# AdaLN, Mamba scan and mixture of experts on one core: the next batch's statistics and its normalization move into the stretch behind scan 2, with scan 3 behind the router's logits

## The chip, the cores and the metric

The kernel runs on one NeuronCore of a Trainium2 chip. The metric is the device time of one execution in microseconds; the kernel is run several times and the median is compared.

Its engines are named as the profile names them: PE (TensorE, matrix products and transposes; PEld are its weight loads), DVE (VectorE), ACT (ScalarE), POOL (GpSimd) and SP (SyncE, which here only issues DMAs). Each engine works through its own queue in order; semaphores tie the queues together.

## The reference

Eight batches of x, 512 rows by 128 columns, all in float32. Each goes through

```python
h = layernorm(x) * (1 + ca) + sa
x = x + ga * mamba(h)
h = layernorm(x) * (1 + cb) + sb
x = x + gb * moe(h)
```

where sa to gb come from a small conditioning product. The Mamba part is

```python
xz = h @ in_proj.T; x, z = split(xz)
u = silu(causal_conv(x) + conv_b)              # 256 channels
dt, Bm, Cm = split(u @ x_proj.T)               # 8 + 16 + 16 columns
delta = softplus(dt @ dt_w.T + dt_b)
s = s * exp(delta * A) + (delta * u) * Bm      # 16 states per channel, over 512 steps
y = sum_n(s * Cm) + u * D
out = (y * silu(z)) @ out_proj.T
```

The expert part has a shared expert and 8 routed ones, of which the two with the highest router probability count, weighted by it:

```python
probs = softmax(flat @ router_w + router_b)
weights = probs where among the top 2, else 0   # a tie goes to the lower index
out = shared(flat) + sum_e weights[e] * expert_e(flat)   # each: gelu(x @ w1 + b1) @ w2 + b2
```

## The kernel before

**Pipeline.** `pipeline` (L293) calls each engine's `slots(b, a, n, m)` for stretches i = 0 to 7. In stretch i the engines scan batch b = i, finish batch a = i − 1 (gate, output projection, experts), prepare batch n = i + 1 (convolution, dt, softplus), and normalize the x of batch m = i + 2. So a and m are both there in stretches 1 to 5; stretch 0 has no a, stretches 6 and 7 have no m. A prologue comes before, a `tail` for the last batch behind.

**Units.** The scan of a batch is 16 units u of 128 partitions by 1024 elements (two states of one half of the channels). For each, VectorE makes the input (`scan_input`, L1197: B row times delta·u, into PSUM), then runs the scan (`scan`, L1206). GpSimd multiplies by C (`readout`, L433), TensorE adds the result to y by transposes (`y_add`, L516). ScalarE makes the decay factors (`decays`, L885, two instructions per unit). Scan u waits for decay u, for its input, and for `y_add` of unit u − 4, whose state buffer it takes (`STATE_RING` 4). `AHEAD` says how many units' decays are made in the stretch before.

**VectorE's queue.** The order is written by hand in `slots` (L1318). Between the units stand the jobs of the other batches:
- `gate_y(a)`, L1216;
- `residual(a)` (L1222: adds attention's rows in PSUM to x, then the statistics of the second normalization);
- `x1hat(a)` (L1238: normalizes; waits for `rstd2_done`);
- `split_h2(a)`, L1310, and `logits(a)` (L1249, three small instructions; waits for the router's product);
- `top2(a)`, L1264, which makes the weights;
- `stats(m)` (L1144; waits for the load of x, `x_in`) and `xhat(m)` (L1155; waits for `rstd_done`);
- `make_delta(n)` (L1163, softplus' sums) behind scan 7, `delta_x(n)` behind scan 12.

**GpSimd's queue.** `slots` (L437) has the last readout of a, then readouts 0 to 14 of b. A readout that is `paced` also waits until the input of the unit after next scan, u + 1, is made. `make_rstd` (two tiny instructions, L420 and L423: add epsilon, power −0.5; called the root below) stands behind readout 2 for a and behind readout 5 for m.

**TensorE's queue** (L700). After the output projection: dt_proj 0, `att_transpose(a)` (L600), dt_proj 1, `y_add` 0 and 1, `keep_busy` (transposes of the identity with no use for the result, L611), `x1_transpose(a)` (L616), `y_add` 2, `keep_busy`, `router(a)` (L624), 18 `up` projections (L645 to L647; the first waits for the split), `y_add` 3, and then `down` products and mixes with the further `y_add`s.

**ScalarE's queue** (L1017). softplus' steps, `softplus_exp`, decays, `h2_rows(a)` (L992, L995: the transposed x1 scaled, read by the split and the router), decays, `router_e`, 18 gelus, `softplus_log`, then mixes and decays in turn.

**SP's queue** (L354). `load_x(m)` (L347) stands behind the store of n's B and C rows to DRAM (L361) and the wait for its landing; these stand behind the end of the preceding stretch. At the end of stretch 1 that is the one-time store of the gate row, and a wait for it:

```python
if b and b.i == 1:
    sp.wait_ge(gate_steps, 4)
    sp.dma_start(gate_dram, gateT[:, 1, B - 1:B]).then_inc(gate_stored, 16)
    sp.wait_ge(gate_stored, 16)
```

**Top 2.** Five instructions of 128 by 256 elements: other = mine, other > mine, the former times a mask of lower indices (`before`), the sum of both, and its reduction to a rank.

## Time and profile before

| what | us |
|---|---|
| median of 3 runs | 687.32 |
| lowest and highest | 684.01, 691.07 |
| the profiled execution | 684.8 |
| its span | 683.1 |
| VectorE busy in it | 598.3 |
| TensorE busy | 593.3 |
| ScalarE busy | 489.7 |
| GpSimd busy | 320.2 |

The profile covers one execution. The span runs from the first to the last recorded instruction; the profiled execution's own time is 1.7 us longer. Times of rows count from the span's start.

### The profile page before, as it was taken

What the parts mean: (1) busy time and instruction counts of PE and PEld (TensorE: products, weight loads), DVE (VectorE), ACT (ScalarE), POOL (GpSimd) and SP (SyncE); (2) the same over time, 40 slices, a digit from 0 to 9 for tenths busy, and PEclk for the clock granted to TensorE, in tenths of its full rate; (3) what the DMA queues carried; (4) which work ended last, traced back from release to release, by engine and by line L of the source; (5) the groups of instructions that cost most, each with busy time, mean ns of one, the idle gap of its engine ahead of it and who ended that gap; (6) DMA issues with size and microseconds to landing.
All of it is one profiled execution on the core that took longest, in us unless ns stands there. A gap on an engine that the chain in (4) does not pass through costs nothing.

```text
span 683.1 us, 9767 instructions
## 1 busy us (share of the span) xinstructions
PE 593.3 (87%) x3646; PEld 466.5 (68%) x3646; DVE 598.3 (88%) x713; ACT 489.7 (72%) x861; POOL 320.2 (47%) x171
## 2 busy tenths in 40 slices
PE   5684478899989998999989998999979947998897
PEld 4243345689657965788567966787668936798686
DVE  5399999999999999999999999999998999798416
ACT  3689535999589976989589957998598925962460
POOL 1036556446654556446653656446543664464000
PEclk9787589999999999999999999999999968999999
DMA  7423333314432235133531343223522442220000
GB/s 221 161 92 140 123 139 142 125 70 169 163 128 82 108 128 184 62 124 124 173 124 63 124 160 138 83 103 124 179 103 70 176 156 83 103 78 16 1 1 16
DMA packets 26705, 77.87 MB, mean 114 GB/s; under 512 B 3025, under 2 KB 17570, under 8 KB 18466
## 3 DMA queue, kind: packets, MB, share of 16 engines
q1 hardware_dynamic: 26178, 76.82, 31.1%
q8 instruction: 29, 0.48, 0.3%
q10 hardware_dynamic: 480, 0.43, 0.2%
q14 instruction: 18, 0.15, 0.1%
HBM read 74.61 MB, written 2.62 MB: 113 GB/s over the span
## 4 chain that ended last, share of the span: by engine, by line
PE 53%; DVE 31%; issue 7%; ACT 5%; POOL 2%; DMA 1%; DVEq 0%; POOLq 0%; ACTq 0%
DVE state L1206 15%; PE psum L677 12%; PE psum L516 10%; DVE psum L1197 8%; PE psum L543 5%; PE psum L645 5%; PE psum L647 4%; PE psum L646 4%; PE psum L687 3%; POOL state L433 2%; PE psum L662 2%; PE psum L565 1%; ACT L866 1%; DVE out_sb L1244 1%; PE psum L799 1%
## 5 line engine op out<-in xcount | busy, mean ns | idle before, releaser
L433 POOL TENSOR_TENSOR state<-state,bc 128x1024 f32<-128x1024 f32 x127 | 300.1, 2363 | 291.8 <-DVE psum L1197 291.8
L1206 DVE TENSOR_TENSOR_SCAN state<-decay,psum 128x1024 f32<-128x1024 f32 x128 | 292.2, 2283 | 21.9 <-PE psum L516 9.5
L885 ACT ACTIVATE decay<-delta,a_neg 128x511 f32<-128x511 f32 x256 | 166.1, 729 | 10.4 <-DVE state L1206 10.3
L516 PE MATMUL psum<-ident,state 128*128 128x128 f32 x1024 | 139.0, 283 | 33.6 <-POOL state L433 33.4
L1197 DVE TENSOR_TENSOR psum<-bc,du 128x1024 f32<-128x1024 f32 x128 | 157.6, 1231 | 4.8 <-DVE state L1206 0.5
L516 PEld LDWEIGHTS psum<-ident,state 128*128 128x128 f32 x1024 | 120.3, 146 | 56.0 <-POOL state L433 44.9
L677 PE MATMUL psum<-down_w,h 128*128 128x128 f32 x896 | 109.9, 276 | 0.0
L677 PEld LDWEIGHTS psum<-down_w,h 128*128 128x128 f32 x896 | 104.4, 192 | 5.3 <-issue 5.3
L1014 ACT ACTIVATE h<-psum,vec 128x512 f32<-128x512 f32 x144 | 97.0, 688 | 2.1 <-PE psum L647 0.6
L980 ACT ACTIVATE gT_mix<-psum,w 128x128 f32<-128x128 f32 x224 | 64.8, 388 | 20.0 <-PE psum L687 14.4
L645 PE MATMUL psum<-h_hi,up_hi 128*128 128x512 f32 x144 | 59.2, 411 | 10.7 <-DVE h_lo L1310 6.7
L543 PE MATMUL psum<-h_sb,conv_in_wT 128*128 128x512 f32 x128 | 59.9, 614 | 8.8 <-ACT h_sb L895 8.8
L647 PE MATMUL psum<-h_hi,up_lo 128*128 128x512 f32 x144 | 57.7, 401 | 0.0
L646 PE MATMUL psum<-h_lo,up_hi 128*128 128x512 f32 x144 | 57.6, 400 | 0.0
L543 PEld LDWEIGHTS psum<-h_sb,conv_in_wT 128*128 128x128 f32 x128 | 24.3, 199 | 34.6 <-issue 25.4
L645 PEld LDWEIGHTS psum<-h_hi,up_hi 128*128 128x128 f32 x144 | 27.5, 191 | 20.5 <-DVE h_lo L1310 7.3
L687 PE MATMUL psum<-ident,gT_mix 128*128 128x128 f32 x224 | 33.9, 274 | 0.0
L647 PEld LDWEIGHTS psum<-h_hi,up_lo 128*128 128x128 f32 x144 | 27.4, 190 | 6.7
L646 PEld LDWEIGHTS psum<-h_lo,up_hi 128*128 128x128 f32 x144 | 27.6, 191 | 6.0
L687 PEld LDWEIGHTS psum<-ident,gT_mix 128*128 128x128 f32 x224 | 26.0, 141 | 1.5 <-ACT gT_mix L980 1.5
L611 PE MATMUL psum<-ident 128*128 128x128 f32 x210 | 26.2, 273 | 0.0
L906 ACT ACTIVATE du<-psum,vec 128x512 f32<-128x512 f32 x16 | 10.8, 687 | 21.2 <-PE psum L543 18.7
(151 smaller groups left out, 638.3 us busy)
## 6 DMA issues: line engine op xcount, KB each, us to landing
bc<-bc_rows SPq DMA_DIRECT2D x64, 1024.0 KB, 4.7
x_sb<-_attn_hidden_states_dram SPq DMA_DIRECT2D x9, 256.0 KB, 2.8
x<-_attn_hidden_states_dram SPq DMA_DIRECT2D x7, 256.0 KB, 3.0
out_dram<-out_sb SPq DMA_DIRECT2D x7, 256.0 KB, 2.4
h<-in_L_ffn_rw_dram SPq DMA_DIRECT2D x1, 1024.0 KB
bc_rows<-rows SPq DMA_DIRECT2D x8, 64.0 KB, 4.8
h<-in_L_wmod_dram ACTq DMA_DIRECT2D x1, 384.0 KB
h<-in_L_attn_in_proj_w_dram SPq DMA_DIRECT2D x1, 256.0 KB, 4.7
```

Source lines behind the costliest of these rows:

```text
L433: pool.tensor_tensor(state[:, u % STATE_RING, :, :], state[:, u % STATE_RING, :, :], bc[:, pair % BC_RING, 1, first:first + NU, :], ALU.mu ...
L516: last = nc.tensor.matmul(Y[q][:, t * P:(t + 1) * P], state[:, u % STATE_RING, s, t * P:(t + 1) * P], ident[:, :], start=False, stop=(u in ...
L543: last = nc.tensor.matmul(A[q], conv_in_wT[:, q, k, :], h_sb[:, k:k + L], start=(k == 0), stop=(k == KC - 1))
L645: nc.tensor.matmul(bank, high, h2_hi[:, :], start=True, stop=False)
L646: nc.tensor.matmul(bank, high, h2_lo[:, :], start=False, stop=False)
L647: nc.tensor.matmul(bank, low, h2_hi[:, :], start=False, stop=True).then_inc(up_done, 1)
L677: last = nc.tensor.matmul(A[j % 2][:, e * DM:(e + 1) * DM], h1[:, (group * EG + e) * HQ + q, ts], down_w[:, group * EG + e, q, :], start=( ...
L687: last = nc.tensor.matmul(OUTP[:, t * P:(t + 1) * P], mix[:, j % 2, e, :], ident[:, :], start=False, stop=(j == DOWNS - 1 and e == EG - 1) ...
L885: last = nc.scalar.activation(decay[:, r, s, 1:L], delta[:, b.p, q, 1:L], ACT.Exp, scale=a_neg[:, q, k:k + 1])
L1014: nc.scalar.activation(h1[:, m, :], UP_RING[m % 3], ACT.Gelu, bias=vec[:, bias:bias + 1]).then_inc(gelu_done, 1)
L1197: nc.vector.tensor_tensor(IN, bc[:, pair % BC_RING, 0, first:first + NU, :], du[:, b.p, q:q + 1, :].broadcast_to([P, NU, L]), ALU.mult).th ...
L1206: nc.vector.tensor_tensor_scan(state[:, u % STATE_RING, :, :].rearrange("p n t -> p (n t)"), decay[:, u % DECAY_RING, :, :].rearrange("p n ...
```

## The change

On VectorE, where both a and m are there, `stats(m)` moves from ahead of scan 6 to behind `residual(a)`, and `xhat(m)` from behind scan 6 to behind input 3. `x1hat(a)` stands ahead of input 3, and split and logits ahead of scan 3. Without m the order of a's jobs changes alike; without a nothing does. The two statistics get buffers of their own (`bn_in`).

On GpSimd readout 2 isn't paced where there is an a, and the root for m follows the one for a. On TensorE `att_transpose` comes ahead of dt_proj 0, `y_add` 2 ahead of `x1_transpose`, and `keep_busy` has other counts. On ScalarE seven units' decays are made ahead, and one fewer pair before the gelus. `top2` has three large instructions, not five: mine is scaled by 1 − 2^-24 where the other's index is lower, and one comparison counts both kinds.

```diff
-AHEAD = 6
+AHEAD = 7
...
         bn = sb("bn", [P, NT, 6])
+        bn_in = sb("bn_in", [P, NT, 6])
...
                     if b:
-                        readout(b, u)
+                        readout(b, u, paced=not (a and u == 2))
                     if a and u == 2:
                         make_rstd(1, stats2_done, rstd2_eps, rstd2_done, a)
-                    if m and u == 5:
+                    if m and u == (2 if a else 5):
                         make_rstd(0, stats_done, rstd_eps, rstd_done, m)
...
+                if a:
+                    att_transpose(a)
                 if n:
                     dt_proj(n, 0)
-                if a:
-                    att_transpose(a)
-                if n:
                     dt_proj(n, 1)
...
-                if a:
-                    keep_busy(a, n, 14)
+                    y_add(b, 2)
+                if a:
+                    keep_busy(a, n, 8)
                     x1_transpose(a)
-                if b:
-                    y_add(b, 2)
-                if a:
-                    keep_busy(a, n, 5 if b else 12)
+                    keep_busy(a, n, 10)
                     router(a)
...
                 if b:
                     decays(b, AHEAD)
+                if a:
+                    h2_rows(a)
+                if b:
                     decays(b, AHEAD + 1)
-                if a:
-                    h2_rows(a)
-                if b:
-                    decays(b, AHEAD + 2)
-                    decays(b, AHEAD + 3)
...
-                    if b and j < DOWNS - 2:
-                        decays(b, AHEAD + 4 + j)
+                    if b:
+                        decays(b, AHEAD + 2 + j)
...
-                nc.vector.tensor_tensor(gt_eq[:, 1, :, :, :], other, mine, ALU.is_equal
-                                        ).then_inc(prob_step, 1)
-                nc.vector.tensor_tensor(gt_eq[:, 0, :, :, :], other, mine, ALU.is_gt
-                                        ).then_inc(prob_step, 1)
+                nc.vector.tensor_tensor(
+                    gt_eq[:, 1, :, :, :], pr[:, :, :].unsqueeze(3).broadcast_to([P, NT, E, E]),
+                    tie_scale[:, :, :].unsqueeze(1).broadcast_to([P, NT, E, E]),
+                    ALU.mult).then_inc(prob_step, 1)
+                dve.wait_ge(prob_step, k + 4)
+                nc.vector.tensor_tensor(
+                    gt_eq[:, 0, :, :, :], pr[:, :, :].unsqueeze(2).broadcast_to([P, NT, E, E]),
+                    gt_eq[:, 1, :, :, :], ALU.is_gt).then_inc(prob_step, 1)
                 dve.wait_ge(prob_step, k + 5)
-                nc.vector.tensor_tensor(
-                    gt_eq[:, 1, :, :, :], gt_eq[:, 1, :, :, :],
-                    before[:, :, :].unsqueeze(1).broadcast_to([P, NT, E, E]),
-                    ALU.mult).then_inc(prob_step, 1)
-                dve.wait_ge(prob_step, k + 6)
-                nc.vector.tensor_tensor(gt_eq[:, 0, :, :, :], gt_eq[:, 0, :, :, :],
-                                        gt_eq[:, 1, :, :, :], ALU.add).then_inc(prob_step, 1)
...
                     scan_input(b, 2)
                     scan(b, 2)
+                if a:
+                    residual(a)
+                if a and m:
+                    stats(m)
+                if a:
+                    x1hat(a)
                 if b:
                     scan_input(b, 3)
-                if a:
-                    residual(a)
+                if a and m:
+                    xhat(m)
+                if a:
+                    split_h2(a)
+                    logits(a)
                 if b:
                     scan(b, 3)
-                if a:
-                    x1hat(a)
-                if b:
                     scan_input(b, 4)
                     scan(b, 4)
-                if a:
-                    split_h2(a)
-                    logits(a)
-                if b:
                     scan_input(b, 5)
                     scan(b, 5)
                 if a:
                     top2(a)
                 if b:
                     scan_input(b, 6)
-                if m:
+                if m and not a:
                     stats(m)
                 if b:
                     scan(b, 6)
-                if m:
+                if m and not a:
                     xhat(m)
```

## Rows read from the trace of the kernel before

**Rows 1.** The page: busy us of each engine (share); the scans (busy, mean ns | idle before).

```profile
PE 593.3 (87%) x3646; PEld 466.5 (68%) x3646; DVE 598.3 (88%) x713; ACT 489.7 (72%) x861; POOL 320.2 (47%) x171
...
L1206 DVE TENSOR_TENSOR_SCAN state<-decay,psum 128x1024 f32<-128x1024 f32 x128 | 292.2, 2283 | 21.9 <-PE psum L516 9.5
```

**Rows 2.** Timeline of VectorE in stretch 4: start, duration, line, operation.

```profile
339.78 2.29 DVE L1206 TENSOR_TENSOR_SCAN state<-decay,psum 128x1024 f32<-128x1024 f32 x1
...
343.25 0.69 DVE L1226 TENSOR_TENSOR x<-psum,x 128x512 f32<-128x512 f32 x1
...
345.18 2.25 DVE L1206 TENSOR_TENSOR_SCAN state<-decay,psum 128x1024 f32<-128x1024 f32 x1
347.35 1.09 DVE L1244 TENSOR_SCALAR out_sb<-x,mean_var,rstd 128x128 f32<-128x128 f32 x4
...
351.92 0.67 DVE L1310 TENSOR_TENSOR h_lo<-h,h_hi 128x512 fp32r<-128x512 f32 x1
...
353.05 1.23 DVE L1197 TENSOR_TENSOR psum<-bc,du 128x1024 f32<-128x1024 f32 x1
...
356.61 0.16 DVE L1268 TENSOR_REDUCE router_stats<-gT_mix 128x4 f32<-128x32 f32 x1
...
359.52 1.23 DVE L1197 TENSOR_TENSOR psum<-bc,du 128x1024 f32<-128x1024 f32 x1
360.65 0.86 DVE L1147 BATCH_NORM_STATS2 bn<-x_sb 128x6 f32<-128x128 f32 x4
...
361.85 2.26 DVE L1206 TENSOR_TENSOR_SCAN state<-decay,psum 128x1024 f32<-128x1024 f32 x1
364.51 1.12 DVE L1158 TENSOR_SCALAR x_sb<-x_sb,mean_var,rstd 128x128 f32<-128x128 f32 x4 [0.40 <-POOL rstd L423]
...
367.29 2.29 DVE L1206 TENSOR_TENSOR_SCAN state<-decay,psum 128x1024 f32<-128x1024 f32 x1 [0.52 <-PE psum L516]
...
375.29 2.29 DVE L1206 TENSOR_TENSOR_SCAN state<-decay,psum 128x1024 f32<-128x1024 f32 x1
...
378.98 2.29 DVE L1206 TENSOR_TENSOR_SCAN state<-decay,psum 128x1024 f32<-128x1024 f32 x1
```

**Rows 3.** Groups by line: one of top2's large instructions (count | busy, mean ns | idle before).

```profile
L1288 DVE TENSOR_TENSOR gT_mix<-gT_mix 128x256 f32<-128x256 f32 x8 | 3.4, 425 | 0.3
```

**Rows 4.** Timeline of GpSimd in stretch 4: readout 2 and the power of the root.

```profile
343.42 2.38 POOL L433 TENSOR_TENSOR state<-state,bc 128x1024 f32<-128x1024 f32 x1 [1.34 <-DVE psum L1197]
...
346.03 1.01 POOL L423 TENSOR_TENSOR rstd<-rstd,constants 128x4 f32<-128x4 f32 x1
```

**Rows 5.** Timeline of TensorE in stretch 4: attention's transpose and the router.

```profile
341.61 0.66 PE L600 MATMUL psum<-ident,h 128*128 128x128 f32 x4
...
350.69 1.06 PE L624 MATMUL psum<-router_sb,h 128*128 128x8 f32 x8
```

**Rows 6.** Timeline of SP's DMA issues; the page's row on x's loads (KB, us to landing).

```profile
183.78 0.43 SPq L385 DMA_DIRECT2D gate_row<-gateT  x1
193.36 0.32 SPq L387 DMA_DIRECT2D gate_row_sb<-gate_row  x1
...
198.81 0.38 SPq L347 DMA_DIRECT2D x_sb<-_attn_hidden_states_dram  x1
...
416.61 0.39 SPq L347 DMA_DIRECT2D x_sb<-_attn_hidden_states_dram  x1
...
x_sb<-_attn_hidden_states_dram SPq DMA_DIRECT2D x9, 256.0 KB, 2.8
```

**Rows 7.** Timeline of VectorE in stretch 2: scan 2.

```profile
189.56 2.29 DVE L1206 TENSOR_TENSOR_SCAN state<-decay,psum 128x1024 f32<-128x1024 f32 x1
```

**Rows 8.** The page: the decays.

```profile
L885 ACT ACTIVATE decay<-delta,a_neg 128x511 f32<-128x511 f32 x256 | 166.1, 729 | 10.4 <-DVE state L1206 10.3
```

**Rows 9.** Two windows: length, busy of each engine, granted clock (PEclk), DMA share, GB/s.

```profile
546.00:552.00 6.00, 2.70 (x20) 2.14 (x20) 5.80 (x4) 4.33 (x7) 3.71 (x2) 1.00 0.08 33
552.00:560.00 8.00, 3.23 (x15) 2.69 (x14) 7.70 (x6) 0.00 (x0) 4.68 (x2) 0.55 0.58 194
```

## What the change should do to the time

> **What bounds the kernel now.** I first read the busy line of the page [rows 1]: VectorE (DVE) 598.3 us and TensorE (PE) 593.3 us of a span of 683.1 us. A share can't say which of the two holds the other, so I read VectorE's timeline of one period, the stretch in which batch 4 is scanned [rows 2]. Scan 2 ends there at 339.78 + 2.29 = 342.07 and scan 7 starts at 367.29, that is 25.22 us later. In between VectorE stands still only twice: 0.40 us ahead of the normalization of x (L1158), for GpSimd's root, and 0.52 us ahead of scan 7, for TensorE. The reader is to see that everything else on that engine touches: an instruction that waits for nothing starts some 0.08 us before the one ahead of it ends, a scan 1.36 us after the start of its own input (1.23 long). Five such pairs repeat at 3.69 us from scan to scan (375.29 to 378.98). For 16 units per batch that is 59 us of a period of 75.1 (from scan 2 of stretch 2, 189.56 [rows 7], to that of stretch 4, halved); the rest is side work on the same queue. So in the middle of the run VectorE is the bound, and a change is worth what it takes off VectorE's queue less what it makes that queue wait. The start and the end, where other engines set the pace, are untouched here.
>
> Eight stretches i = 0 to 7 scan one batch each. The change acts where a batch is finishing (a) beside one being scanned (b): i = 1 to 7. In i = 1 to 5 there is also a batch whose x is prepared (m); in 6 and 7 there is none. All times below count from the end of scan 2.
>
> **The change, part by part: a stretch with m.**
>
> *Residual.* attention's transpose (L600) ends at 341.61 + 0.66 = 342.27 behind half of dt_proj [rows 5]; put ahead of it, it ends about 0.2 earlier, at 0.0. The residual, formerly behind input 3, can start at 0.1. Its block lasts 345.18 − 343.25 = 1.93, so it ends at 2.04.
>
> *Next x's statistics.* They last 361.85 − 360.65 = 1.20 and reach 3.24.
>
> *The root.* GpSimd's readout 2 no longer waits for input 3 (it could not: input 3 now stands behind the root) and starts at 0.1. From a readout's start to the end of the root behind it is 346.03 + 1.01 − 343.42 = 3.62 [rows 4], so x1hat starts at 3.74. The statistics fill 1.2 of that wait and 0.5 remains: a wait that was not there.
>
> *Scan 3 behind split and logits.* Before, scan 4 and input 4 covered the way x1hat, transpose, h2, router, logits. The way takes from x1hat's start 347.35 to the router's end 350.69 + 1.06 = 351.75, i.e. 4.40, and 0.04 to wake VectorE [rows 2, 5]. What is left in front of logits is x1hat 1.00 (1.09 long, overlapped), input 3 1.13, xhat 1.03 (1.12) and the split 0.58 (0.67): 3.74. So split and logits wait 0.7 in all and logits start at 3.74 + 4.44 = 8.18. Split and logits together took 353.05 − 351.92 = 1.13, logits 0.55 of it, so scan 3 starts at 8.73. ScalarE has one pair of decays ahead of h2 rather than two, so h2 isn't held.
>
> *The rest.* Scans 4 and 5 at 12.42 and 16.11, top2 2.20 behind at 18.31. top2's block lasted 359.52 − 356.61 = 2.91. It loses one operation that overlapped its neighbour (0.42 − 0.08 = 0.34) and one that waited for its predecessor (0.425 + 0.04 = 0.46) [rows 3]: 0.80 less, so input 6 starts at 20.42, scan 6 at 21.79, scan 7 at 25.48. Scan 7 no longer waits for TensorE: the up projections start some 2.7 earlier, and so does the readout's sum behind them.
>
> Result: 25.48 against 25.22, **+0.26 per stretch**. The 0.80 of top2 and the 0.92 of two old waits are paid back by 1.2 of new ones, and by lost overlaps: three scans, not one, are followed directly by their next input, and one more scan stands directly behind its input. Bounds: −0.2 (both new waits 0.25 shorter), +0.5.
>
> *Decays.* AHEAD = 7 shifts one pair (2 × 0.729 = 1.5 at most, [rows 8]) from behind softplus to the end of the preceding stretch, and one more pair into the stretch of the mixes. There they are covered: ScalarE starts its gelus about 2 earlier. If that cover were gone, TensorE's chain to gate_y would be late by up to 1.5 per stretch. I take 0 and keep +0.5 per stretch for the range. keep_busy (14 + 5 becomes 8 + 10) lies in TensorE's idle time: 0.
>
> *Stretches 6 and 7.* Without m there is nothing to fill: x1hat still starts at 3.74, so scan 7 still at 25.48. Before, these two lacked 1.20 + 1.03 + 0.40 of work and wait, but stood for TensorE instead: of the 9.5 us for PE in seven waits [rows 1], five like the one shown leave 6.9 for these two, 3.4 each. So before they were at about 25.2 − 2.6 − 0.5 + 3.4 = 25.5. Change: 0, within ±1.5 for both.
>
> **Where the new order meets a transfer.** stats(m) used to run at 360.65, 18.6 us behind scan 2, and now at 2.04. It needs x, which SP loads only after it has stored and seen landed the B and C rows. I read SP's queue for each stretch [rows 6]. In stretch 2 (b.i = 1 came before) SP stood from 183.78 to 193.36 for the one-time store of the gate row, so x is issued at 198.81 and lands 2.8 later, at 201.6. Scan 2 ends there at 189.56 + 2.29 = 191.85 [rows 7]. x is there at 9.8, and VectorE wants it at 2.04. Queued behind it on VectorE are x1hat, input 3 and everything else. x1hat starts at 9.8 + 1.2 = 11.0 instead of 3.74: **+7.3**, once. The other four loads are issued earlier. The latest of them, at 416.61, lands at 419.4; scan 2 ends in that stretch one period (75.1) behind 342.07, so x is there at 2.3, 0.2 late, which the wait for the root covers.
>
> While VectorE stands, TensorE does too, for 7 us. In the trace TensorE was busy 2.70 of the 6 us up to 552, at a granted clock of 1.00 (2.4 GHz), and the mean over the next 8 us was 0.55, nearly all of it at the lower level, 1.2 GHz [rows 9]. A full stop of 7 us should do the same: then x1's transpose (0.66) and the router (1.06), both on the way to logits, take up to twice as long: up to 1.7, I take 1.2. The Trainium skill (TensorE: Matmul & The Clock Gate, § Part 1: The HAM clock gate) likewise says that an idle array falls back to 1.2 GHz; at a clock that stayed up, the sum would be 1.2 lower.
>
> **Sum.** 4 stretches × 0.26 = 1.0; stretch 2: 7.3 + 0.26 + 1.2 = 8.8; stretches 6 and 7: 0; start and end: 0 (in the end top2 is covered by TensorE's projections). **+9.8 us.** The profiled execution took 684.8 us, its span 683.1 with 1.7 around it; it becomes 694.6. That execution lies 2.5 below the median of the runs shown, 687.3, to which I add the same: **697.1 us**, 1.4% slower.
>
> **Rivals.**
>
> *GpSimd held by VectorE.* The root for x now runs beside x1hat and input 3. In the rows before, roots ran beside scans only ([rows 4] beside 345.18). If x1hat and input 3 hold GpSimd off, the power (1.01) starts at about 6.1, xhat at 7.15, split at 8.2, logits at 8.8, scan 3 at 9.35: +0.6 in five stretches, total +12.9: 700.2. For it: the code paces every readout to avoid input rows. Against it: operands of four elements. The Trainium skill (SBUF — State Buffer, § Who interferes with whom) says that a VectorE instruction with two SBUF inputs, or in a two-port mode, excludes a GpSimd instruction that reads SBUF. By that rule it comes out this way; no row here shows the overlap.
>
> *A shorter stop in stretch 2.* The gate row is 0.5 KB and landed 9.6 us after its issue [rows 6], once, in one execution. If in other executions it takes no longer than the x load, 2.8, x is there 6.8 earlier, at 3.0: the stop shrinks to 0.5 and the clock stays up. Total 5 × 0.26 + 0.5 = +1.8: 689.1. A landing of 6.5 gives +6.7, 694.0, the edge of what is within 1%. For it: the trace has this store once. Against it: nothing that runs ahead of it on SP is changed.
>
> *Gain.* If the way to logits were covered and x there in time in every stretch, the new waits of 0.5 + 0.7 go: 25.48 becomes 24.3, 0.9 below before: 5 × 0.9, and 0.8 of top2 in two more stretches: −6.1: 681.2, near the edge of faster by 1%. It decides on one row: x's load in stretch 2 must be there at 2.0, and 198.81 speaks plainly against it. Even without that stop, the root and router rows keep the balance at +1.
>
> *Late engines.* ScalarE's extra decays make TensorE's chain late by 0.5 in five stretches: +12.3: 699.6.
>
> **How the numbers follow.** Forecast (+8 to +11) 0.42; GpSimd held 0.20; late engines 0.08; shorter stop or none 0.18; gain 0.07; something else, split evenly, 0.05. About 1% is what a measurement of this kernel can tell from no change: 6.9 us, so the bounds are 680.4 and 694.2. Slower by over 1%: forecast, held and late, 0.70, of which the spread of runs takes a little and half of something else gives some back: 0.68. Faster: half of the gain case, and a part of something else: 0.05. Within 1%: the rest, 0.27. Range: the lower end holds the shorter stop with the spread of the runs shown (3.5), 690; the upper end the held case with it, 703.
>
> **What would show it.** In the profile after: the first instruction of x's statistics in stretch 2 waits some 7.5 us for the DMA of x; x1hat waits 0.5 for GpSimd and logits 0.5 for the router in stretches 1, 3, 4 and 5; no wait of scan 7 for TensorE; top2 2.1 long; the distance from scan 2's end to scan 7's start 25.5. If that wait in stretch 2 is missing, the forecast is wrong by its largest term. If the distance is 26 or more with xhat waiting for the root, the second case holds. If gate_y waits over 0.5 for TensorE, the decays were not hidden.

## The result, and the profile after

The changed kernel is slower: median 702.1 us (701.4 to 706.0, 4 runs) against 687.5 us (684.0 to 691.1) of the kernel before; ratio 1.0231, 95% interval 1.0187 to 1.0276, that is 15.9 us (12.9 to 19.0). I had forecast 9.8 us. The direction and its largest term were right; the size was too small by over a third.

The page of the changed kernel, busy us and scans, to be held against [rows 1]:

```profile
span 700.0 us, 9730 instructions
...
PE 602.8 (86%) x3639; PEld 474.9 (68%) x3639; DVE 595.5 (85%) x697; ACT 490.3 (70%) x861; POOL 320.1 (46%) x171
...
L1203 DVE TENSOR_TENSOR_SCAN state<-decay,psum 128x1024 f32<-128x1024 f32 x128 | 292.5, 2285 | 14.2 <-DVE psum L1194 0.5
```

VectorE has 2.8 us less to do, and the scans' idle time fell from 21.9 to 14.2 us: no scan 7 waits for TensorE now. Yet the span grew by 16.9 us. The groups of waits of VectorE say what it waits for instead (in total, times, longest; the large waits of start and end left out):

```profile
DVE bn_in L1144 <- DMA x_sb<-_attn_hidden_states_dram: 9.3, 2, 6.7
DVE h_lo L1301 <- ACT h_hi L994: 8.3, 7, 2.2
...
DVE gT_mix L1251 <- PE psum L626: 7.5, 8, 3.3
DVE out_sb L1241 <- POOL rstd L425: 5.9, 7, 1.6
```

In the kernel before, x's load held VectorE for 2.9 us in all, the router 3.3, the root ahead of x1hat 1.4, all in the start and the end, and h2 not at all. x's load (L1144), h2 (L1301), the router (L1251) and the root (L1241) are the four places at which the new order waits.

**Stretch 4** of the changed kernel, VectorE's timeline, answers [rows 2]. Scan 2 ends at 352.22 + 2.29 = 354.51.

```profile
352.22 2.29 DVE L1203 TENSOR_TENSOR_SCAN state<-decay,psum 128x1024 f32<-128x1024 f32 x1
354.61 0.69 DVE L1223 TENSOR_TENSOR x<-psum,x 128x512 f32<-128x512 f32 x1
...
358.22 1.12 DVE L1241 TENSOR_SCALAR out_sb<-x,mean_var,rstd 128x128 f32<-128x128 f32 x4 [0.42 <-POOL rstd L425]
359.25 1.23 DVE L1194 TENSOR_TENSOR psum<-bc,du 128x1024 f32<-128x1024 f32 x1
360.39 1.11 DVE L1155 TENSOR_SCALAR x_sb<-x_sb,mean_var,rstd 128x128 f32<-128x128 f32 x4
362.00 0.69 DVE L1301 TENSOR_TENSOR h_lo<-h,h_hi 128x512 fp32r<-128x512 f32 x1 [0.51 <-ACT h_hi L994]
363.12 0.19 DVE L1251 TENSOR_TENSOR gT_mix<-psum,router_bias 128x32 f32<-128x32 f32 x1 [0.43 <-PE psum L626]
...
363.67 2.29 DVE L1203 TENSOR_TENSOR_SCAN state<-decay,psum 128x1024 f32<-128x1024 f32 x1
...
380.48 2.29 DVE L1203 TENSOR_TENSOR_SCAN state<-decay,psum 128x1024 f32<-128x1024 f32 x1
```

x1hat starts 3.71 behind scan 2 (forecast 3.74), scan 7 starts at 380.48, 25.97 behind (forecast 25.48, before 25.22). The three waits are where the forecast put them: 0.42 for the root (forecast 0.5), and 0.51 + 0.43 = 0.94 ahead of split and logits together (forecast 0.7). logits start at 363.12 − 354.51 = 8.61, 0.43 later than forecast.

**Stretch 2**: SP's issues, to be held against [rows 6].

```profile
186.48 0.43 SPq L386 DMA_DIRECT2D gate_row<-gateT  x1
195.42 0.32 SPq L388 DMA_DIRECT2D gate_row_sb<-gate_row  x1
...
200.36 0.38 SPq L348 DMA_DIRECT2D x_sb<-_attn_hidden_states_dram  x1
```

VectorE's first instruction of x's statistics, in the timeline of the same stretch:

```profile
203.18 0.87 DVE L1144 BATCH_NORM_STATS2 bn_in<-x_sb 128x6 f32<-128x128 f32 x4 [6.68 <-DMA x_sb<-_attn_hidden_states_dram]
```

The chain of waits of that stretch (start, us, what), which goes back from the projections:

```profile
186.48 8.92 DMA gate_row<-gateT
...
195.78 4.56 DMA bc_rows<-rows
...
200.36 2.80 DMA x_sb<-_attn_hidden_states_dram
...
203.18 0.87 DVE bn_in L1144 x4
```

The three transfers follow each other with at most 0.4 between them, as the forecast had it. Scan 2 ended there at 194.38; scan 7 starts 33.29 behind it, 8.05 more than in the kernel before (25.24).

Stretch by stretch, the distance from scan 2's end to scan 7's start, from the two profiled executions (us):

| stretch | 1 | 2 | 3 | 4 | 5 | 6 | 7 |
|---|---|---|---|---|---|---|---|
| before | 25.24 | 25.24 | 25.23 | 25.22 | 25.23 | 25.42 | 26.70 |
| after | 28.13 | 33.29 | 27.64 | 25.97 | 25.98 | 25.98 | 26.47 |
| difference | 2.89 | 8.05 | 2.41 | 0.75 | 0.75 | 0.56 | −0.23 |

Together 15.2 of the span's 16.9 us. Stretches 1 and 3 stand out; the next view is theirs. Two pairs of windows of TensorE in the changed kernel, ahead of and around x1's transpose, stretch 3 and stretch 4 (length, busy of PE, PEld, DVE, ACT, POOL, granted clock, DMA share, GB/s):

```profile
272.00:279.00 7.00, 5.98 (x27) 3.12 (x25) 6.66 (x8) 4.40 (x8) 4.74 (x3) 1.00 0.31 110
279.00:283.00 4.00, 4.00 (x22) 3.90 (x22) 3.53 (x19) 3.97 (x7) 3.04 (x5) 0.59 0.00 0
```

```profile
349.00:356.00 7.00, 5.98 (x29) 3.36 (x27) 6.70 (x8) 4.40 (x7) 4.73 (x3) 1.00 0.36 130
356.00:360.00 4.00, 4.00 (x35) 3.66 (x35) 3.49 (x21) 3.97 (x7) 3.29 (x5) 1.00 0.00 0
```

In stretch 3 the granted clock falls to the lower level (1.2 GHz) just where the sums of units 0 to 2 and the fillers stand ahead of x1's transpose; stretch 4 had the same 5.98 us of work in 7 and kept 2.4 GHz. The sums of units 0 to 2 in stretch 3 and in stretch 4:

```profile
279.10 4.50 PE L518 MATMUL psum<-ident,state 128*128 128x128 f32 x24
```

```profile
356.34 2.84 PE L518 MATMUL psum<-ident,state 128*128 128x128 f32 x24
```

They took 1.66 longer, and scan 7 comes just as much later (27.64 − 25.98): in this order the lower clock costs what it adds to this block. x1's transpose (0.60) and the router (1.06) behind it ran as in stretch 4.

### The profile page after: what moved, and what is told of

The parts are those of the page before. It is cut to its first block, busy times and chain, and to the rows that moved or that the text cites. A ratio compares the mean times of both kernels' runs of the same rounds, so it can differ in the third digit from the quotient of the medians.

```text
span 700.0 us, 9730 instructions
## 1 busy us (share of the span) xinstructions
PE 602.8 (86%) x3639; PEld 474.9 (68%) x3639; DVE 595.5 (85%) x697; ACT 490.3 (70%) x861; POOL 320.1 (46%) x171
## 4 chain that ended last, share of the span: by engine, by line
DVE 45%; PE 31%; ACT 9%; issue 7%; POOL 3%; DMA 3%; DVEq 1%; POOLq 0%; SPq 0%; ACTq 0%
DVE state L1203 22%; DVE psum L1194 14%; PE psum L518 5%; PE psum L647 4%; PE psum L648 4%; PE psum L649 4%; POOL state L435 3%; PE psum L595 2%; PE psum L574 2%; PE psum L557 2%; PE psum L626 1%; ACT L956 1%; DMA gate_row<-gateT 1%; DVE delta L1173 1%; DVE delta L1167 1%
## 5 line engine op out<-in xcount | busy, mean ns | idle before, releaser
L1203 DVE TENSOR_TENSOR_SCAN state<-decay,psum 128x1024 f32<-128x1024 f32 x128 | 292.5, 2285 | 14.2 <-DVE psum L1194 0.5
L518 PE MATMUL psum<-ident,state 128*128 128x128 f32 x1024 | 144.1, 291 | 44.2 <-POOL state L435 43.9
L518 PEld LDWEIGHTS psum<-ident,state 128*128 128x128 f32 x1024 | 124.0, 150 | 70.9 <-POOL state L435 57.6
L979 ACT ACTIVATE gT_mix<-psum,w 128x128 f32<-128x128 f32 x224 | 64.0, 371 | 22.2 <-PE psum L689 15.9
L963 ACT ACTIVATE g_soft<-psum 128x1024 f32<-128x1024 f32 x8 | 8.2, 1025 | 25.4 <-PE psum L588 25.4
```

Of the source, the lines that this page charges most:

```text
L518: last = nc.tensor.matmul(Y[q][:, t * P:(t + 1) * P], state[:, u % STATE_RING, s, t * P:(t + 1) * P], ident[:, :], start=False, stop=(u in ...
L979: last = nc.scalar.activation(mix[:, j % 2, e, :], A[j % 2][:, e * DM:(e + 1) * DM], ACT.Copy, scale=w9[:, t, group * EG + e:group * EG + ...
L1203: nc.vector.tensor_tensor_scan(state[:, u % STATE_RING, :, :].rearrange("p n t -> p (n t)"), decay[:, u % DECAY_RING, :, :].rearrange("p n ...
```

## Experiments

Each run starts from the changed kernel unless it says otherwise, and every one of these but "changed, again" has the late gate store too. "The late gate store" is this edit and nothing else:

```diff
-                if b and b.i == 1:
+                if b and b.i == B - 2:
                     sp.wait_ge(gate_steps, 4)
```

The ratios are to the kernel before as it was run beside each (medians 686.1 to 687.6 us). "No fill ahead" has all 18 fillers behind x1's transpose.

| run | median us (range, runs) | ratio to before, 95% |
|---|---|---|
| changed kernel | 702.1 (701.4–706.0, 4) | 1.0231 (1.0187–1.0276) |
| late gate store | 694.1 (692.6–694.5, 4) | 1.0104 (1.0059–1.0149) |
| scan 3 back | 688.2 (686.1–690.7, 10) | 1.0015 (0.9984–1.0047) |
| covered | 691.1 (683.5–696.3, 10) | 1.0040 (0.9995–1.0084) |
| new top2 alone | 685.8 (684.0–689.8, 10) | 1.0006 (0.9977–1.0034) |
| no fill ahead | 693.3 (691.1–695.9, 4) | 1.0116 (1.0073–1.0160) |
| no fill, dt_proj first | 691.1 (690.1–691.9, 5) | 1.0073 (1.0043–1.0103) |
| decays as before | 699.6 (1) | |
| covered, no fill, dt_proj first | 682.2 (681.0–686.2, 10) | 0.9951 (0.9922–0.9980) |
| before, late gate store | 686.9 (683.6–689.6, 10) | 0.9987 (0.9950–1.0024) |
| before, again | 693.1 (1) | |
| changed, again | 700.7 (1) | |

### The gate row's store moved

> The changed kernel with one line moved: SP issues and waits for the gate row's store at the end of stretch 6 (no x is loaded behind it), not of stretch 1. Nothing else changes. Theory (the stop in stretch 2 is the wait for x, and x is late because SP waits for that store): VectorE's 6.68 us wait for the DMA of x is gone, TensorE keeps its clock there, the distance from scan 2's end to scan 7's start falls from 33.3 to the 26.0 of stretches 4 and 5: 7.3 less, total about 694.5. Rival (x is late because of traffic on the DMA queue, whatever SP waits for): the wait stays above 3 us and the total above 698. What is left over the kernel before, about +7, must then be the stretches themselves and TensorE's clock.

Measured: 694.1 us, and the interval of its ratio lies wholly below that of the changed kernel. The difference of the two ratios, 1.27%, is 8.7 us. SP's issues in stretch 2 of this run:

```profile
184.34 0.39 SPq L362 DMA_DIRECT2D bc_rows<-rows  x1
188.98 0.38 SPq L348 DMA_DIRECT2D x_sb<-_attn_hidden_states_dram  x1
```

x is issued 3.2 before scan 2 ends (189.90 + 2.29 = 192.19), not 6.0 behind it (200.36 against 194.38), and VectorE has no wait for it. The theory stands: the stop came from SP's order. The stretch's distance is 27.64, not the 26.0 that I expected: TensorE's clock fell in it, the sums of units 0 to 2 took 4.51, and the wait ahead of the split is 2.19. Stretch 5, at the lower clock too, has 27.65; stretches 3, 4 and 6 have 25.98 to 25.99. Stretch 1 has 26.47 without a fall of the clock: the 0.5 more is a wait of 0.51 ahead of scan 4, which stands in stretch 1 of every version of the new order and for which the profile names nothing but the scan's own input. Its cause stays open. What remains over the kernel before is 1.0%, about 7 us.

### The same move in the kernel before

> The kernel before with the gate row's store at the end of stretch 6. Theory (in the old order x is wanted 18 us behind scan 2, so the store at the end of stretch 1 cost nothing): within 0.3% of the kernel before, no wait for a DMA in its middle. Rival (the store's wait on SP also held B and C rows or the preceding stretch): 1 us or more faster, and then a part of the gain of the last version is not due to its order.

Measured: 0.9987, with 1 inside the interval; the distances are 25.22 to 25.23 in stretches 1 to 5 as before, and no wait for a DMA stands between 100 and 640 us. The store was free as long as x was wanted 18 us behind scan 2. It came to cost 8 us through the new order alone.

### The new top2 alone, in the kernel before

> The kernel before with the new top2 alone (three large instructions instead of five), nothing moved. Theory (in the old order VectorE is held at scan 7 by TensorE's sum of unit 3, and behind it by the logarithm): 0.80 less work per stretch turns into a wait of scan 7 that grows from 0.52 to about 1.3, total within 1 us of the kernel before. Rival (VectorE's work is what counts): 0.8 in seven stretches, 5.6 us less, 682.

Measured: 1.0006. VectorE's timeline in stretch 4 of this run has the row that answers the scan 7 of [rows 2]:

```profile
371.38 2.29 DVE L1207 TENSOR_TENSOR_SCAN state<-decay,psum 128x1024 f32<-128x1024 f32 x1 [1.27 <-PE psum L517]
```

0.52 has become 1.27: of the 0.80 saved 0.75 stands as a longer wait in the same place, and the distance is 25.18 instead of 25.22 in stretches 4 and 5. Stretches 1 to 3 of this profile have 25.93 to 26.00, with waits of 2.0 to 2.1; TensorE was at the lower clock in them. The saving is real and worth nothing in the old order.

### Scan 3 ahead of the split

```diff
                 if a and m:
                     xhat(m)
+                if b:
+                    scan(b, 3)
                 if a:
                     split_h2(a)
                     logits(a)
                 if b:
-                    scan(b, 3)
                     scan_input(b, 4)
```

> As the run with the late gate store, but scan 3 stands between the normalization of x and the split (order: x1hat, input 3, xhat, scan 3, split, logits, input 4). Theory (in the new order VectorE waits on the way x1hat, transpose, h2, router, which nothing covers): the waits of 0.51 ahead of the split and of 0.43 ahead of logits go in stretches 4 to 6, and those of 2.2 in 1 and 3, where TensorE ran at the lower clock, go too. Distance scan 2 to scan 7 about 25.0 in all stretches, total about 685 to 687. Rival (the waits only move, because TensorE's projections start 1 us later and scan 7 waits for the sum of unit 3 again): scan 7 waits 0.3 to 0.6 and the total stays above 690.

Measured: 688.2, 0.9% under the run with the late gate store (694.1). In stretch 4:

```profile
353.33 2.28 DVE L1203 TENSOR_TENSOR_SCAN state<-decay,psum 128x1024 f32<-128x1024 f32 x1
355.59 0.69 DVE L1301 TENSOR_TENSOR h_lo<-h,h_hi 128x512 fp32r<-128x512 f32 x1
356.71 0.19 DVE L1251 TENSOR_TENSOR gT_mix<-psum,router_bias 128x32 f32<-128x32 f32 x1 [0.42 <-PE psum L626]
```

The split follows scan 3 without a wait, although TensorE's clock fell in this stretch, as it did in 1 and 5; in the order of the change the split waits about 2.2 us then. Distances are 25.1 to 25.3 in stretches 3 to 6. It does not hold everywhere: in stretch 2, where TensorE stood at the lower clock for 8 us and not 4, the split waited 1.61 and the distance is 26.88, and in stretch 6, where there is no xhat to cover, it waited 0.77. The total is 1 us above my range: the wait for the router stayed, gate_y now waits 0.44 to 0.63 for TensorE in four stretches, and scan 7 waits 0.58 in stretch 3. So placing scan 3 behind split and logits costs about 0.9% in the new order; that the waits "only move" is refuted for most of the split's and half true for the rest.

### No fillers ahead of x1's transpose

```diff
-                    keep_busy(a, n, 8)
                     x1_transpose(a)
-                    keep_busy(a, n, 10)
+                    keep_busy(a, n, 18)
```

> The changed kernel with the late gate store and all 18 filling transposes behind x1's transpose, none ahead (18 instead of 8 + 10). Theory (the 0.5 that my forecast missed in each stretch is x1's transpose queued on TensorE behind the sums of units 0 to 2 and the 8 fillers): x1's transpose starts when x1hat ends, 0.5 earlier; ScalarE is then held 0.3 by a pair of decays, so split comes 0.2 to 0.3 earlier. Distance scan 2 to scan 7: 25.7 at the full clock, total 1 to 2 us under the run with the late gate store. Rival (TensorE loses its clock without the fillers): stretches at the lower clock in four or more of seven, total 695 or more.

First the two timelines of TensorE at the full clock, the changed kernel (stretch 4) and this run (stretch 4):

```profile
359.01 1.04 PE L613 MATMUL psum<-ident 128*128 128x128 f32 x8
359.89 0.60 PE L618 MATMUL psum<-ident,out_sb 128*128 128x128 f32 x4
```

```profile
346.04 2.84 PE L518 MATMUL psum<-ident,state 128*128 128x128 f32 x24
349.09 0.66 PE L618 MATMUL psum<-ident,out_sb 128*128 128x128 f32 x4 [0.21 <-DVE out_sb L1240]
```

x1hat in this run, on VectorE:

```profile
347.92 1.11 DVE L1240 TENSOR_SCALAR out_sb<-x,mean_var,rstd 128x128 f32<-128x128 f32 x4 [0.42 <-POOL rstd L425]
```

x1hat ended at 358.22 + 1.12 = 359.34 in the one, and the transpose came 0.55 later, behind the fillers. In the other it ended at 347.92 + 1.11 = 349.03 and the transpose followed at 349.09. The distance is 25.69 in stretches 2, 4 and 6, as expected, 0.29 less than 25.98. It is not the whole 0.5: ScalarE's pair of decays now ends 0.3 behind the transpose (350.03 against 349.75), and the 18 fillers end 0.3 behind h2 (351.71 against 351.37), ahead of the router. Stretches 3 and 5, also at the full clock, have 25.85 and 25.87: in 3 VectorE waited 0.57 for x, in 5 it waited 0.46 for attention's transpose. Between scans 2 and 7 TensorE ran at the lower clock in stretch 1 alone. The medians, 693.3 and 694.1, don't tell the two versions apart, and both are above my 1 to 2 us less; only the traces show the 0.29. That y_add 2 was moved ahead of the transpose is not what held it at the full clock: the sums end at 356.34 + 2.84 = 359.18, before x1hat does.

### Half of dt_proj ahead of attention's transpose again

> As the run without the fill ahead, and half of dt_proj stands again ahead of attention's transpose. Theory (moving attention's transpose ahead made softplus, and with it the decays ahead of h2, some 0.4 late; with that undone nothing but the transposes is left on the way): split waits under 0.2, distance 25.5 to 25.7 at the full clock, total 690 to 692. Rival (the residual comes 0.2 later for it, and that is all): distance 25.9 and a wait for attention's transpose of 0.2 ahead of the residual.

Measured: distance 25.70 in stretch 2 and 25.71 in stretch 6, at the full clock, against 25.69 without this edit. The split waits less, but the residual now waits 0.31 for the transpose, and the two cancel. (Stretches 1 and 5, at the full clock too, have 26.13, with the 0.50 ahead of scan 4, and 26.06, where the residual waits 0.66.) My theory of it falls: that move of the change is worth nothing either way at the full clock. (691.1 against 693.3, with intervals that overlap.) Stretches 3 and 4, at the lower clock, have 26.27 and 26.26, only 0.6 over 25.7 and not 1.7: the sums took 4.48 there as well, but no fillers stood between them and the transpose.

### The decays as before

The three edits on ScalarE undone: six units ahead, two pairs of decays ahead of h2, two behind.

> The changed kernel with the late gate store and the decays as in the kernel before: six units ahead, two pairs ahead of h2 and two behind it. Theory (in the new order h2 is on the way that VectorE waits for): the second pair of decays ahead of h2 makes it 1.3 later, so the wait ahead of the split grows from 0.5 to about 1.8 and the one ahead of logits stays 0.4; distance 27.2 in every stretch, total about 702. Rival (seven ahead costs as much at the end of the stretch): the waits at gate_y shrink in return and the total stays near 694.

Measured: 699.6 in a single run. The distance is 26.89 in stretches 2, 4 and 5, 0.9 over 25.98, and the split waits 1.43 instead of 0.51 in 2 and 4. I had expected 27.2; the pair takes 1.3, of which part was idle. The new place of the decays is a part of the change that helps: without it each stretch would be 0.9 longer. Which of the three edits does it was not tried. The forecast's case of late engines (decays at the end of the stretch holding TensorE's chain) is refuted: in stretches 1 to 6 of the changed kernel gate_y starts 0.07 before its predecessor ends, in 2, 3, 5 and 6 of the kernel before 0.10 behind it.

### A version without waits

Late gate store, and VectorE's order:

```diff
                 if a and m:
                     stats(m)
+                if b:
+                    scan_input(b, 3)
                 if a:
                     x1hat(a)
                 if b:
-                    scan_input(b, 3)
+                    scan(b, 3)
+                if a:
+                    split_h2(a)
                 if a and m:
                     xhat(m)
                 if a:
-                    split_h2(a)
                     logits(a)
                 if b:
-                    scan(b, 3)
                     scan_input(b, 4)
```

> A version meant to have no wait on VectorE: late gate store, order residual, statistics of x, input 3, x1hat, scan 3, split, xhat, logits, input 4. Theory: input 3 covers the rest of the wait for the root, scan 3 the transpose and h2, xhat the router. From the durations of the kernel before, the distance from scan 2's end to scan 7's start comes to 24.2 against 25.24: 1.0 less in each of stretches 1 to 5, about as much in 6 and 1 to 2 in 7. Total 679 to 682. Rival (the loop through TensorE and ScalarE is as long as VectorE's, so what VectorE gains comes back as a wait at gate_y, at the softplus steps or at scan 7): total 684 to 688 with such waits of 0.5 to 1 per stretch.

Measured: 691.1, no better than the kernel before, with runs from 683.5 to 696.3. In its profile (683.9 us) stretch 3, at the full clock, has the distance 24.25, as worked out. But stretches 1, 2 and 4, at the lower clock, have 26.14, 25.72 and 25.72, with 1.5 of waiting ahead of the split. With the 8 fillers still queued ahead of it, the way through x1's transpose reaches past its cover as soon as TensorE slows down. gate_y waits 0.42 to 0.50 for TensorE in stretches 3 to 6, as the rival said.

The same with the fillers behind x1's transpose and half of dt_proj first (two edits together):

> The version meant to have no wait on VectorE (input 3 ahead of x1hat, scan 3 ahead of the split, xhat ahead of logits), with half of dt_proj ahead of attention's transpose and all fillers behind x1's transpose. Theory: the lower clock costs less, because TensorE has less queued ahead of x1's transpose: distance 24.3 at the full clock and at most 25 at the lower one; gate_y still waits 0.4 for the loop through TensorE. Total 682 to 685, ahead of the kernel before by 0.2 to 0.6%. Rival (the loop through TensorE and ScalarE sets the period): no better than the first such version, 686 and more.

Measured: 682.2 us, ratio 0.9951 (0.9922 to 0.9980), 0.5% under the kernel before and the only version whose interval lies wholly below 1. VectorE's timeline in stretch 4:

```profile
343.01 1.20 DVE L1194 TENSOR_TENSOR psum<-bc,du 128x1024 f32<-128x1024 f32 x1
344.13 1.10 DVE L1241 TENSOR_SCALAR out_sb<-x,mean_var,rstd 128x128 f32<-128x128 f32 x4
345.15 2.27 DVE L1203 TENSOR_TENSOR_SCAN state<-decay,psum 128x1024 f32<-128x1024 f32 x1
347.46 0.69 DVE L1301 TENSOR_TENSOR h_lo<-h,h_hi 128x512 fp32r<-128x512 f32 x1
348.07 1.11 DVE L1155 TENSOR_SCALAR x_sb<-x_sb,mean_var,rstd 128x128 f32<-128x128 f32 x4
349.09 0.18 DVE L1251 TENSOR_TENSOR gT_mix<-psum,router_bias 128x32 f32<-128x32 f32 x1
```

Not one wait in these rows: input 3 covers the root, scan 3 the transpose and h2, xhat the router. (Ahead of them the residual waits 0.31 for attention's transpose.) The distance is 24.44 to 24.45 in stretches 2 to 4, 24.82 in 1 and 24.80 in 5, where scan 4 and the residual wait. Of the 0.8 gained per stretch, gate_y gives a part back, with a wait of 0.45:

```profile
332.49 1.23 DVE L1213 TENSOR_TENSOR gT_mix<-psum,z_silu 128x1024 f32<-128x1024 f32 x1 [0.45 <-PE psum L518]
```

The sum of unit 15 sets that point now, as the rival said in part. What the lower clock does to this version its profile shows once only, in stretch 6: the sums took 4.50, the split had no wait, and the distance is 24.29. Stretches 1 to 5 kept the full clock, so the expected "at most 25" was not put to the test there.

### Both kernels profiled a second time

> The kernel before, unchanged, for a second profile. Question: the first profile shows no stretch at the lower TensorE clock near x1's transpose, most of the changed versions do. Theory (where such a stretch falls differs from execution to execution, in the old order too; what the order sets is its price): one to three of them here as well, each costing VectorE under 0.9 us, at scan 7. Rival (the old order never loses the clock there): none.

> The changed kernel, unchanged, for a second profile. Theory: the wait for x in stretch 2 is 6 to 7.5 us again, since it hangs on SP's order; stretches at the full clock have the distance 26.0 again; the stretches at the lower clock are others than 1 and 3, each with a distance near 27.7. Rival (the lower clock is bound to stretches 1 and 3): the same ones.

The kernel before, second profile, 693.1 us: the lower clock falls into stretches 1, 2 and 3, where the first profile had none. Scan 7 of stretch 3:

```profile
296.23 2.29 DVE L1206 TENSOR_TENSOR_SCAN state<-decay,psum 128x1024 f32<-128x1024 f32 x1 [1.27 <-PE psum L516]
```

Distances 26.12, 25.96 and 25.98 instead of 25.23: 0.7 to 0.9 each. The changed kernel, second profile, 700.7 us: the wait for x is 7.38, stretches 3 to 6 have 25.97 to 25.99, and the lower clock fell in 1 and 2, not in 3. So the lower clock is not bound to the new order, nor to stretch 3 (in stretch 1 it was there both times).

The windows show two places at which it falls, and the order sets the price of each. Some 1 to 2 us behind scan 2, over the sums of units 0 to 2, it costs 1.66 in the order of the change. In the old order it fell there in stretch 1 of the second profile, and the distance is 26.12 against 25.96 in stretch 2, which had only the later fall: some 0.2. Some 10 us behind scan 2, over the up projections, it costs the old order 0.7, as a longer wait of scan 7. In the order of the change it cost nothing there: the run with the decays as before had it in stretches 2 and 5, with the same 26.89 as stretch 4 without it. The few profiles don't say how often the clock falls; that stays open.

## Where the forecast held and where it failed

The sum of the forecast against the two first profiles (16.9 us of span):

| term | forecast | measured |
|---|---|---|
| stretch 2 | +8.8 | +8.05 |
| stretches 1, 3, 4, 5, at the full clock | 4 × 0.26 = 1.0 | 4 × 0.75 = 3.0 |
| lower clock in stretches 1 and 3 | 0 | 2 × 1.66 = 3.3 |
| wait ahead of scan 4 in stretch 1 | 0 | 0.5 |
| stretches 6 and 7 | 0 | +0.3 |
| everything else | 0 | +1.7 |

The median, 702.1, lies near the upper end of my range, 703. That is luck as far as the mechanism goes: that end stood for GpSimd held by VectorE, which did not happen; TensorE's clock and queue filled the gap.

**The stop in stretch 2: right, in place, cause and size.** Seen in the row of L1144, and shown by moving one line: 8.7 us less, and nothing in the kernel before. x1hat came 6.3 later than in stretch 4 (forecast 7.3). The clock's part was mis-sized by little: the lower clock did come, x1's transpose took 1.11 instead of 0.66, the router 1.72 instead of 1.06, and logits waited 1.47 for it instead of 0.43, that is 1.0 more (forecast 1.2).

**"keep_busy lies in TensorE's idle time: 0": wrong.** This is the first step that failed. I took the way from x1hat to logits, 4.44, from the old order, where TensorE stood idle ahead of x1's transpose. In the new one x1hat comes 1.6 us earlier (5.28 behind scan 2 before, 3.71 now), while the sums of units 0 to 2, one of them newly moved ahead of the transpose, and 8 fillers still run. The way measured 363.12 − 358.22 = 4.90: 0.46 more, in each stretch at the full clock. I had priced what the transpose depends on, not what was queued ahead of it on its engine. The run without the fillers ahead shows the transpose following x1hat at once; that gave back 0.29 of the 0.49 by which the stretch exceeded 25.48. The other 0.2 is decays ahead of h2 and fillers ahead of the router, read from rows and not tried by a run.

**The lower clock was priced only behind the stop.** The first profile of the kernel before showed TensorE at 2.4 GHz between scans 2 and 7 of stretches 1 to 6, and I took that for the rule. The second shows that it isn't. In the old order scan 4 and input 4 covered the way, so that a fall over the sums ahead of x1's transpose cost some 0.2; the new order took the cover away, and pays 1.66, the whole of what the sums take longer (4.50 instead of 2.84). That is the second failed step, and the larger in us: a cover was removed, and its price was worked out for one clock only. How much of it is due to y_add 2, which the change also put ahead of the transpose, no run separates.

**The root, statistics and top2: right.** x1hat at 3.71 (forecast 3.74), top2 2.12 long (373.32 to 375.44; forecast 2.11), no wait of scan 7.

**Stretches 6 and 7: +0.3 for 0, in part by luck.** I had 25.48 after the change in each and 25.5 before. Measured were 25.98 and 26.47 after, 25.42 and 26.70 before: in stretch 7 both sides were 1.0 to 1.2 too low, and the errors cancel.

**Rivals.** GpSimd held by VectorE: not in the changed kernel. The power for x ran from 358.44 to 359.45, its usual 1.01, beside x1hat, and xhat had no wait. Late engines: refuted, gate_y waits less than before. A shorter stop: the two profiles have 6.68 and 7.38. The gain: the last version without waits shows what its condition was worth, 24.4 per stretch, and to keep it at the lower clock too the order on TensorE had to change.

**Open.** The 1.7 us elsewhere are a sum of parts: 0.2 less ahead of the first of these stretches, 1.1 less between scan 7 and the next scan 2, and 3.0 more behind scan 7 of stretch 7. In that last part gate_y of the last batch waited 2.88 and 2.81 in the two profiles of the changed kernel and 1.18 in both of the kernel before, with the lower clock at that point in the former. Why it falls there was not tried; the run with the late gate store had no fall there, and its gate_y waited 1.24. The last batch's mixes waited for TensorE 14.64 in the changed kernel and 12.37 in the first profile of the kernel before, but 15.1 in two others of the old order: those 2.3 us can't be put down to the change. Nor was it settled how much of the median's 15.9 us is the lower clock: profiles show where it fell in single executions.

## What to carry to other kernels

When work moves earlier on the engine that sets the time, look up for each of its inputs not only when it was ready but by how much its producer could have been asked for it sooner: the x load came 6.7 us late in one stretch of five, and the transpose 0.5 short behind fillers that used to be free. A saving on that engine is worth nothing while it waits for another one in the same period (top2: 0.80 saved, 0.75 more waiting). Put the longest instructions that need nothing, here a scan, over the longest way through other engines; an order with slack there also pays less when TensorE's clock falls (0.2 against 1.66 here). One profile that shows no fall of the clock doesn't say that there is none.

## What the runs showed of the hardware that I had not expected

**VectorE can hold a tiny GpSimd instruction.** In the version without waits the first step of x's root (add epsilon, 4 elements per partition) runs beside input 3, which reads two operands from SBUF. Its group in the changed kernel and in that version (count | busy us, mean ns):

```profile
L422 POOL TENSOR_TENSOR rstd<-mean_var,constants 128x4 f32<-128x4 f32 x16 | 3.2, 202 | 34.7 <-DVE mean_var L1149 20.0 <-DVE mean_var L1232 14.6
```

```profile
L422 POOL TENSOR_TENSOR rstd<-mean_var,constants 128x4 f32<-128x4 f32 x16 | 9.1, 569 | 27.9 <-DVE mean_var L1149 14.3 <-DVE mean_var L1232 13.6
```

and its timeline in stretch 4 of the latter:

```profile
343.25 1.01 POOL L422 TENSOR_TENSOR rstd<-mean_var,constants 128x4 f32<-128x4 f32 x1
344.34 1.01 POOL L425 TENSOR_TENSOR rstd<-rstd,constants 128x4 f32<-128x4 f32 x1
```

0.20 us became 1.01, ending at 344.26, 0.05 behind input 3 (343.01 + 1.20 = 344.21). It was so in all of stretches 1 to 5 (1.00 to 1.01), and in 6 and 7 the root for a, beside input 3 there, took 1.19 and 1.09. In the changed kernel all 16 took 0.20 or 0.21. The power behind it, beside x1hat (344.13 to 345.23), took its usual 1.01. So the rule of the Trainium skill (SBUF — State Buffer, § Who interferes with whom) that a VectorE instruction with two SBUF inputs shuts out a GpSimd instruction that reads SBUF agrees with this row. On its other half, VectorE instructions in a two-port mode, no row here decides: x1hat did not hold the power, but no row shows in which mode x1hat ran. It cost nothing, since the root for x was ready at 344.34 + 1.01 = 345.35 and xhat came at 348.07; in the order of the change the step ran ahead of input 3 and took 0.20.

**TensorE's clock fell with TensorE busy.** In stretch 3 of the changed kernel it had worked 5.98 of the 7 us up to the fall to the lower level, as in stretch 4, where it did not fall. I had expected a fall only behind a stop. Of two profiles of the kernel before, one has no fall between scans 2 and 7 of stretches 1 to 6, the other has falls in stretches 1, 2 and 3. Their spans, 683.1 and 690.2 us, differ by 7.1, about as much as its timed runs (684.0 to 691.1). Of this, 2.5 stands ahead of the scans (idle 21.9 and 24.4), and 4.5 in two waits outside these stretches (12.4 and 15.1 for TensorE, 7.7 and 9.5 for ScalarE), the first of them with TensorE at the lower clock from 649 to 657 us in the second profile and not in the first; the cause was not tried.
